# Attention stage of a two-layer kernel: maxima in twos, products' low parts on GpSimd, the mix two units later

## What is computed

```python
qkv = x @ attn_qkvw + attn_qkvb            # 1024 x 1536
q, k, v = per head, 16 wide, 32 heads
scores = jnp.einsum('bhqd,bhkd->bhqk', q, k) * scale
probs = jax.nn.softmax(scores, axis=-1)
ctx = jnp.einsum('bhqk,bhkd->bhqd', probs, v)
return ctx @ attn_ow + attn_ob
```

## Time and profile before

| | |
|---|---|
| median of 3 runs | 1622.95 us (1622.28 to 1625.58) |
| the profiled execution | 1626.14 us |
| its span | 1624.2 us |
| TensorE, VectorE, ScalarE, GpSimd busy | 93%, 64%, 50%, 14% |
| mean granted TensorE clock | 0.961 of full |
| products in `mha_heads` | 1108.4 to about 1202 us |
| units, first score to last mix | 1204.48 to 1541.57 us |
| output projection and linear layer | 1547.1 us to the end |

### The profile page before, as it was taken

One profiled execution on the slowest core, in us unless ns is written; L12 is line 12 of the kernel. 1 busy time (PEld: TensorE's weight loads), 2 busy tenths in 40 slices (PEclk: granted clock), 3 DMA queues, 4 the chain that ended last, 5 costly groups with the idle time before them and its releaser, 6 DMA issues. The chain is left out here.

```text
span 1624.2 us, 22378 instructions
## 1 busy us (share of the span) xinstructions
PE 1502.8 (93%) x8030; PEld 991.4 (61%) x8030; DVE 1038.6 (64%) x2048; ACT 810.8 (50%) x1467; POOL 232.0 (14%) x233
## 2 busy tenths in 40 slices
PE   6867999999999999959979999898999999999987
PEld 4645776666777676647868887786553333333264
DVE  5744666666666666644643433564888999999245
ACT  5325666666666666641221221222117777777834
POOL 2762111112111111100000000001000122331200
PEclk9977999999999999989979999998989999999999
DMA  4142221212122221134212110117420222320001
GB/s 137 53 191 72 85 69 63 69 63 69 63 92 76 69 69 40 34 103 162 97 53 77 59 59 20 52 50 186 148 27 14 72 74 76 77 66 15 18 14 46
DMA packets 63298, 116.83 MB, mean 72 GB/s; under 512 B 12830, under 2 KB 32414, under 8 KB 61902
## 3 DMA queue, kind: packets, MB, share of 16 engines
q1 hardware_dynamic: 59956, 106.63, 20.6%
q10 hardware_dynamic: 3168, 8.65, 2.1%
q0 software_dynamic: 64, 0.11, 0.0%
HBM read 83.04 MB, written 29.66 MB: 69 GB/s over the span
## 5 line engine op out<-in xcount | busy, mean ns | idle before, releaser
L1681 DVE TENSOR_REDUCE ah_minus_half<-ah_ring 128x1 f32<-128x512 f32 x512 | 319.7, 679 | 40.3 <-PE ah_ring L1578 40.0
L968 DVE CUSTOM_DVE_ANT_0 mh_score<-mh_score,mh_mask 128x128 f32<-128x128 f32 (+7 forms) x256 | 195.8, 765 | 179.4 <-PE mh_score L781 179.3
L1641 ACT ACTIVATE ah_probs<-ah_score 128x1024 f32<-128x1024 f32 x256 | 248.7, 1023 | 114.6 <-PE ah_score L1595 113.6
L890 ACT ACTIVATE mh_probs<-mh_score,mh_minus_max 128x128 f32<-128x128 f32 (+7 forms) x256 | 189.6, 741 | 39.8 <-DVE mh_minus_max L968 35.8
L1578 PE MATMUL ah_ring<-ah_k_stack,ah_q_stack 48*128 48x512 f32 x512 | 187.1, 468 | 14.1 <-DVE ah_minus_half L1681 4.2
L1578 PEld LDWEIGHTS ah_ring<-ah_k_stack,ah_q_stack 48*128 48x128 f32 x512 | 82.8, 190 | 176.9 <-DVE ah_minus_half L1681 161.5
L1595 PE MATMUL ah_score<-ah_q_stack,ah_k_stack 49*128 49x512 f32 x512 | 158.1, 445 | 3.8 <-DVE ah_v L1705 2.3
L779 PE MATMUL mh_score<-shared,h_hi 128*128 128x512 f32 (+3 forms) x384 | 152.2, 396 | 3.0 <-ACT mh_probs L890 2.9
L1041 POOL TENSOR_TENSOR h_lo<-mh_pe,h_hi 64x512 fp32r<-64x512 f32 x64 | 81.9, 1279 | 459.0 <-ACT h_hi L876 455.4
L1610 PE MATMUL ah_mix<-ah_probs,ah_v 128*32 128x512 f32 x1024 | 139.0, 615 | 0.6 <-ACT ah_probs L1641 0.6
L781 PE MATMUL mh_score<-shared,h_lo 128*128 128x512 f32 (+3 forms) x384 | 133.0, 346 | 0.0
(11 more groups left out here) (222 smaller groups left out, 2854.7 us busy)
## 6 DMA issues: line engine op xcount, KB each, us to landing
mh_w<-in_w_pairs SPq DMA_DIRECT2D x16, 896.0 KB, 5.6
x<-in_w_inner SPq DMA_DIRECT2D x14, 768.0 KB, 4.1
pe_scratch<-fr_pe_out SPq DMA_DIRECT2D x4, 2048.0 KB, 6.6
mh_pe<-pe_scratch SPq DMA_DIRECT2D x16, 512.0 KB, 4.0
mh_spread<-inverse_scratch SPq DMA_DIRECT2D x64, 128.0 KB, 2.9
a_scratch<-mh_mixed SPq DMA_DIRECT2D x32, 256.0 KB, 2.4
x<-a_scratch SPq DMA_DIRECT2D x8, 1024.0 KB, 6.9
qk_scratch<-ai_ring SPq DMA_DIRECT2D x32, 256.0 KB, 2.7
```

What stands on the lines that cost most here:

```text
L890: nc.scalar.activation(probs[:, s % 2, 0:width], score_ps[s % 2][:, base:base + width], ACT.Exp, bias=minus_max[:, s % 4:s % 4 + 1], scale ...
L968: nc.vector.tensor_tensor_reduce(out=scores, in0=scores, in1=mask[:, S - width:S], scale=-1.0, scalar=3e38, op0=ALU.add, op1=ALU.min, accu ...
L1641: nc.scalar.activation(probs[:, 2 * (u % 2) + c, :], score_ps[c][:].rearrange("p e n -> p (e n)"), ACT.Exp, scale=MHA_SCALE).then_inc(prob ...
L1681: nc.vector.reduce_max(minus_half[:, m:m + 1], ring[:, m % 3, :], AX.X, negate=True).then_inc(max_taken, 1)
```

## The change

- **Maxima in twos.** `two_maxima` issues two together and waits until the reduction before the last is done (`max_taken` at least m - 1), still with three banks. Beside products 8 to 23 stand six maxima (two after step 0, two after steps 1 and 2, two after step 3), so 96 are done before the units; the other 416 go over units 0 to 115: 92 units have four, 24 have two, 12 none.
- **Order of a unit:** [second pair of the previous unit], first score, first pair, mix of the unit two before, second score. Three pairs of buffers of probabilities instead of two.
- **Products:** from product 4 on ScalarE takes the bank twice, once in the matmul format and once in full (new buffer `full`), and GpSimd subtracts; GpSimd also makes the weights' lower parts from piece 2 on; ScalarE copies v; the v bias is added after the division, on GpSimd.
- **DMAs:** SyncE reloads the stacks, twelve at a time, once per group; after loading the first stack it waits for its landing before it stores more products.
- Outputs of a half group go into one buffer per half; ScalarE copies them one unit later.

```diff
     def take_upper(self, act, n):
...
+        if n >= 4:
+            wait(act, self.lo_ready, n - 7)
+            self.nc.scalar.activation(self.full[:, n % 4, :], self.bank(n), ACT.Identity, bias=self.bias[:, row:row + 1]
+                                      ).then_inc(self.full_ready, 1)
...
+    def take_lower(self, pool, n):
+        pool.wait_ge(self.hi_ready, n + 1)
+        pool.wait_ge(self.full_ready, n - 3)
+        self.nc.gpsimd.tensor_tensor(self.ring[:, n % 4, 1, :], self.full[:, n % 4, :], self.ring[:, n % 4, 0, :].bitcast(F32),
+                                     ALU.subtract).then_inc(self.lo_ready, 1)
+        pool.wait_ge(self.lo_ready, n - 3)
...
+        self.nc.gpsimd.tensor_scalar(self.c[rows, cols], self.c[rows, cols], self.bias[rows, 2 * ND + k:2 * ND + k + 1], None, ALU.add
+                                     ).then_inc(self.multiplied, 1)
...
-        FIRST = 5 * (products.COUNT - FROM)
-        AHEAD = 6
+        FIRST = 6 * (products.COUNT - FROM)
+        AHEAD, INVERTED = 4, 7
...
-            return min(FIRST - (-unit * (TOTAL - FIRST) // (UNITS - NT - AHEAD)), TOTAL)
+            return min(FIRST - 2 * (-unit * (TOTAL - FIRST) // (2 * (UNITS - NT - AHEAD))), TOTAL)
...
-            now, then = maxima_at(n), maxima_at(n + 1)
-            return (now, min(now + (then - now + 1) // 2, then), min(now + (3 * (then - now) + 2) // 4, then))[stage]
+            return maxima_at(n) if stage == 0 else min(maxima_at(n) + 2, maxima_at(n + 1))
...
+            def reload_stacks(g, row_halves):
+                wait(sp, scores_ready, 2 * NUNIT * (g - DEPTH + 1))
+                load_stacks(sp, g, row_halves)
...
             load_stacks(sp, 0, (0,))
+            sp.wait_ge(stacks_in[0], 16 * (STACK_DMAS + 2))
...
                 shares.put(sp, g - 1, 1, out, out_taken)
+                if DEPTH <= g + 2 < GROUPS:
+                    reload_stacks(g + 2, range(2))
                 put_max(g, 1)
...
+            for job in range(products.NQK):
+                if job >= 4:
+                    products.take_lower(pool, job)
+                for i in pieces.get(job, ()):
+                    products.lower(pool, i)
+                    pool.wait_ge(products.w_ready, i + 1)
...
-            def one_maximum(m):
-                wait(pe, max_taken, m - 2)
-                maximum(m).then_inc(max_ready, 1)
+            def two_maxima(m):
+                wait(pe, max_taken, m - 1)
+                for n in range(2):
+                    maximum(m + n).then_inc(max_ready, 1)
...
-                for part in range(2):
-                    products.product(pe, n, range(2 * part, 2 * part + 2))
+                for part, steps in enumerate(((0,), (1, 2), (3,))):
+                    products.product(pe, n, steps)
...
-            for n in range(UNITS + 1):
+            for n in range(UNITS + 2):
                 for stage in range(3):
                     while done < maxima_before(n, stage):
-                        one_maximum(done)
-                        done += 1
+                        two_maxima(done)
+                        done += 2
+                    if n >= 2 and stage == 1:
+                        mix((n - 2) // NUNIT, (n - 2) % NUNIT)
                     if n < UNITS and stage < 2:
                         scores(n // NUNIT, n % NUNIT, stage)
-                    if n and stage == 2:
-                        mix((n - 1) // NUNIT, (n - 1) % NUNIT)
...
-                wait(act, mixed, NUNIT * g + u - 1)
-                nc.scalar.activation(probs[:, 2 * (u % 2) + c, :], score_ps[c][:].rearrange("p e n -> p (e n)"),
+                wait(act, mixed, NUNIT * g + u - 2)
+                nc.scalar.activation(probs[:, 2 * ((NUNIT * g + u) % 3) + c, :], score_ps[c][:].rearrange("p e n -> p (e n)"),
...
+            for t in range(NT):
+                act.wait_ge(products.ready, products.NQK + t + 1)
+                nc.scalar.copy(v[t][:].rearrange("p (h r) -> p h r", h=H)[:, :, 0:HD],
+                               products.bank(products.NQK + t).rearrange("p (h r) -> p h r", h=H)).then_inc(products.v_ready, 1)
...
-                    if 1 <= u <= STACK_DMAS and DEPTH <= g + 2 < GROUPS:
-                        load_one(g + 2, u - 1)
-                    if u == 0 and g:
+                    if u == 1 and g:
                         take_out(g - 1, 1)
-                    if u == NT:
+                    if u == NT + 1:
                         take_out(g, 0)
```

114 lines of the change are left out of this document (51 added, 63 removed).

## The result

The changed kernel takes **1671.13 us**, the median of four runs (1667.48 to 1682.52), against 1623.59 (1622.28 to 1625.58) for the kernel before on the same chip: a ratio of 1.030 with a 95% interval of 1.0254 to 1.0347. The prediction was 1640 us with a range of 1618 to 1653: the right side, but 31 us short and out of the range. The profiled execution took 1668.05 us; its span is 1666.2, 42.0 above the span of before (1624.2). Where one execution of a kernel lies more than 1.5% above its fastest, the ratios here leave it out.

The account below looks back on a forecast made before the run. It took the ring of three banks, where TensorE and VectorE wait for each other, as the bound. Terms 19.9 + 6.9 - 1.4 - 7.2 - 1.5 + 0.6 = +17.3 on 1626.1 profiled gave 1643.4, predicted as 1640 us; range 1618 to 1653.

Parts of the forecast that it names:

- The units: Second attention: 2.93 us per unit with two pairs, 1.89 with one; +21.1 us, and +19.9 for the whole stage.
- the pair is one grain larger while the ring is not: Units with two pairs: reason given why TensorE's 0.7 idle before the second pair and VectorE's after it stay unhidden.
- the signs named: Profile after: two-pair units 2.9, VectorE waiting some 45 us for maxima, TensorE 0.7 idle before the second pair, products 4.7.
- Rival 1: Units: VectorE never runs dry, units 2.42 and 1.89, total time 1593 us; a gain below 2.74 per unit; chance 0.11.
- Hidden work, (c): SyncE's stack loads in bursts of 12, about 5 us, ahead of the maxima's put: priced at nothing.
- The first stack: Products 8 and 9: wait of 3.31 us and the half clock behind it taken as gone, -7.2 us.
- rival 4: Products 8 and 9: first stack lands no sooner, wait moves to SyncE, half clock stays; 1647 us, no chance given.
- Products 10 to 22: A product with six maxima in three pairs 4.72 us, +6.9 over 16; lower parts moved off VectorE, -1.4.
- The passage: Last maxima of the products to first score: ScalarE copies v, idle about 0.9 instead of 2.35, -1.5 us.
- The table load: Exponential's table behind the last copy of v: 1.28, 0.7 hidden, +0.6; with the skill's drain +1.9, sum 1.3 higher.
- Hidden work (a) and (b): GpSimd's lower parts, memsets and bias additions; ScalarE's 12 more passes in the products, 60 fewer DMA issues: priced at nothing.
- Rival 3, the clock: Units: TensorE's clock falls from idling 0.7 of 2.93; one stretch per group costs 32, total time 1672 us; chance 0.07.

Follow-up runs that it names:

- experiment 2: Changed kernel with SyncE putting the second half's maxima ahead of its burst of twelve stack loads: 1648.24 us, ratio 1.0164.
- experiment 10: Version with pairs and the mix of the previous unit last (puts first), with the second pair behind both scores instead of between them: 1618.61 us, ratio 0.9962.
- experiment 3: As experiment 1, but each maximum of a pair waits for its own bank: 1653.13 us, ratio 1.0194.
- experiment 13: Puts first, single maxima, three ahead of both scores, the fourth behind; seven maxima beside each of the last 15 products, from product 9: 1614.95 us.
- experiment 14: Puts first, three maxima, both scores, fourth maximum, mix; six maxima beside each product from product 9 on, 90 ahead of the units: 1610.83 us, ratio 0.9922.
- experiment 15: As experiment 14, but six and seven maxima by turns beside products from product 9 on, 97 ahead of the units: 1610.63 us, ratio 0.9921.
- experiment 9: Maxima beside products as in experiment 15; unit order two maxima, first score, whole mix of two units before, two maxima, second score: 1651.62 us, ratio 1.0173.
- experiment 11: As experiment 9, but the mix in two halves of 256 columns, each between two pairs of maxima: 1627.88 us, ratio 1.0005.
- experiment 6: Puts-first version of experiment 2, pairs kept, but the mix of the previous unit at the unit's end: 1639.75 us, ratio 1.0118.
- experiment 5: Puts-first version of experiment 2 with the earlier kernel's unit order: single maxima, mix of the previous unit at the end: 1615.48 us, ratio 0.9957.
- experiment 1: Changed kernel with stack loads back on ScalarE's queue, two behind each of units 1 to 6: 1652.46 us, ratio 1.0195.
- experiment 7: Puts-first version of experiment 2 with maxima issued singly, the mix of two units before still between the scores: 1639.96 us, ratio 1.0103.
- experiment 4: As experiment 1, with the earlier kernel's unit order: single maxima, mix of the previous unit at the end: 1638.6 us, ratio 1.01.

## Why the prediction was wrong

By its own steps, in their order.

*The units.* The length was right, 2.93 and 1.89 predicted, 2.95 and 1.90 measured, and the stage without the late puts is 354.0 us for a predicted 354.9 (experiment 2). The reason, "the pair is one grain larger while the ring is not", was wrong: the prediction's own sum holds the score's 0.33 behind the mix, and that, not the pair, is the difference (experiment 10). That the stage's sum holds to 1 us is in part luck: the half clock at the start, left as it was in the sum, lasted 6.8 us where it had lasted 17.1 (from 1203.8 to 1220.9; the 14.70 of the earlier trace rows lie in it), and the extra stretch at 1316 gave most of that back. Of the signs named, the waits of VectorE for maxima came to 71.2 us for 45, and 49.2 with the puts first; the idle of TensorE ahead of the second pair was 0.55 for 0.7. Rival 1 (VectorE never dry, 1593 us) is refuted by the unit of 2.95, far above 2.74; that the stricter wait is the cause is refuted by experiment 3.

*Hidden work, (c): the step that failed.* "SyncE gets the stacks in bursts of 12, about 5 us, ahead of the put of the second half's maxima, the inverses and the weights; the maxima are needed 5 units, 13 us, later", priced at nothing. I priced the burst by its issue time on SyncE's queue. What a put behind it waits for is its bytes: 13.6 us at 116 GB/s, and in the group shown the last part landed 14.4 us after the burst's first issue. TensorE asked for the maxima 11.9 us after that issue, and the four puts landed 15.0 us after it, 6.7 us after their own last issue, where it is 1.0 with the puts ahead (experiment 2). In each of the five groups with a burst that was 1.7 to 4.3 us too late: 16.2 us of TensorE idle. The rest of the 22.9 us that experiment 2 gave back goes with the half clock behind each wait (34.0 us in five stretches against 6.8 in one). In numbers: predicted for the stage +19.9, measured +42.1, miss 22.2. Without the late puts the changed kernel takes 1648.24, inside the range. The other 6 us of the 31 between 1640 and 1671.13 are no step of the sum: the profiled execution of before was 3.2 above its median, that of the changed kernel 3.1 below.

*The first stack: mis-sized too.* I took 7.2 us off for the wait and its half clock, because the loads would have the DMA engines to themselves. They were issued at 1115.7 and had landed at 1127.9, 12.2 us later; before it was 11.8 (issued at 1117.76, landed at 1129.59; the earlier trace rows has the wait). So keeping other loads back did not bring them in sooner: in the 16 profiles of kernels that do so it is 10.3 to 13.9 us, 12.1 in the mean. The wait was 4.55 us and 6.8 us at half clock followed, so products 8 and 9 took 16.40 us for a predicted 9.5. This was rival 4, told as "1647, inside the range"; by itself it is what happened. What does shorten the wait is to ask for the stack later: with the first maximum at product 9 it was 0.95, 2.90, 2.53, 1.47 and 0 us (experiments 13, 14, 15, 9, 11), and 3.2 to 6.8 in the changed kernel and all runs that start at product 8.

*Products 10 to 22:* 61.00 us, 4.69 each, for 4.72 predicted. *The passage:* the first score waited 0.24 us for the copy of v, not 0.9, and the last product with the passage took 5.0 us instead of 6.2. *The table load:* it took 1.28 us and the first exponential came right behind it.

```profile
1204.25 0.59 ACT L1689 COPY ah_v<-ah_score 128x512 f32<-128x512 f32 x1 [4.09 <-PE ah_score L1308]
1204.85 1.28 ACT L1676 ACT_TABLE_LOAD   x1
...
1206.15 1.02 ACT L1676 ACTIVATE ah_probs<-ah_score 128x1024 f32<-128x1024 f32 x1
```

From 1204.85 to 1206.15 it is 1.30 us. The drain that the Trainium skill tells of ("ScalarE: Activation LUTs", section "What ACT_TABLE_LOAD costs") would have shown ahead of the load or behind it, and does not: the copy ends at 1204.84, and the load starts at 1204.85. This was 1.3 us of the other sum.

*Hidden work (a) and (b)* was hidden: no row of the waits names GpSimd's lower parts or ScalarE's passes as what TensorE's products waited for between 1138.9 and 1199.9, where it is busy 61.00 of 61.00 us.

*Rival 3, the clock,* named the time, 1672, and not the cause. The clock did fall in five groups, as it priced, but each time within a wait for the puts or at most 1.0 us behind it; with the puts first one stretch is left (experiment 2), and with pairs alone or the order of before none between the start and the last maximum (experiments 6 and 5). It is not the puts alone: experiments 1 and 3 keep three and two stretches, all but one of 3.4 us, with no wait for the puts. The small idle of 0.55 that each unit has does not bring it down: pairs alone (experiment 6) have 0.54 in most units and the clock at 1.00 from 1220.4 to 1558.3. That speaks against the Trainium skill's rule for short idles ("TensorE: Matmul & The Clock Gate", section "A second HAM failure mode: psum-queue depth-cycling") in its plain form; the one stretch of experiment 2, behind 6 us in which small waits left TensorE busy for 3.91, and the two of experiment 1 at block ends are what such a rule would look like here.

The misses sum to the whole: stage 22.2, products 8 and 9 6.9, the remaining products and passage -1.6, parts not touched -2.8 gives 24.7, and the profiled execution was 42.0 above that of before where the sum said 17.3.

**What each part of the change costs,** by medians of the runs:

| version | us | step |
|---|---|---|
| order of before, puts ahead of the burst | 1615.48 | |
| + pairs, both scores between them | 1618.61 | +3.1 |
| + second pair moved between the scores | 1639.75 | +21.1 |
| + mix of two units before, between the scores | 1648.24 | +8.5 |
| + puts behind the burst (the changed kernel) | 1671.13 | +22.9 |

The rows come from different batches, in which the kernel before ran at 1622.8 to 1625.2, and the ratios to it give 0.8, 25, 7.5 and 22 us for the four steps: a step holds to some 4 us, and the first is not clear of noise. The steps also hold in this order only: the mix's place alone, on singles, cost 24 us (experiment 7). The kernel before lies above the first two rows. What makes that difference (16 maxima more beside the products, ScalarE without DMA issues, GpSimd's share of the lower parts, the copies of v) was not taken apart. In its stage, 320.7 us against 335.0, 16 maxima fewer in the units explain 16 x (2.70 - 2.12) = 9.3 us as an estimate from the earlier trace rows; a start at half clock of 10.2 us for 17.1 in these two profiles would be up to 3.4 more. A sixth maximum beside 16 products, at 4.69 for 4.40 us, costs 4.6 us of it again.

## What to carry to other kernels

Price a burst of DMAs by its bytes over the rate that the trace shows, not by the time in which its queue issues it: here transfers of 2 KB issued behind it on its queue landed only when those bytes were through. So put the small transfer that something waits for ahead of the bulk one, even at the cost of the bulk. Where two engines work through a ring of banks, as here with three, a round of the ring costs its latency whatever stands inside it, as long as that fits in, and all that stands outside it is added: put the small work inside, and let only what is too long for it stand outside. An order is judged by that sum, not by the grain of its hand-overs.

## What was not expected of the hardware

- A put of 2 KB took 6.7 us from its issue behind 1.5 MB on its own queue, and 16 us where a second queue's 1.5 MB and 512 KB of its own were in flight. With nothing bulky ahead on its queue it took 1.0 us. Moving the stack's loads to another engine's queue freed the puts in experiment 1, where they were issued two per unit, and did not in experiment 4, where other bulk stood ahead of them.
- In the stage of the changed kernel a stop of TensorE of 1.7 to 4.3 us was followed each time by 3.4 to 10.2 us at a granted 0.50. The stops cost 16.2 us; the other 7 or so of experiment 2's 22.9 us are the slow stretches, 34.0 us of them against 6.8.
- The first stack's 1.5 MB landed no sooner for keeping back what is issued behind it: 11.8 us with another stack's loads 6 us behind, 10.3 to 13.9 without, from kernel to kernel.
